# Factors split ahead, loads ordered behind the first gathers, row sums by halves: one change to a fused two-layer kernel

## The reference

```
s = L0_attn(xn)                      # spectral attention: normalise, cumsum, product
g = silu(L0_ffn(xn))                 # 64 experts, top 8, capacity 64, F = 96
x = x + s * g
xn = layernorm(x)
s = xn + lora_attention(rms(xn))     # 16 heads of 128, window 64, rotary
g = silu(L1_ffn(xn))                 # 16 experts, top 4, and a shared expert
x = x + s * g
```

```
h @ W.T + h @ A.T @ B.T * (1 / 16)   # rank 16; q, k, v and o
```

## Time and profile before

| | us |
|---|---|
| median of 3 runs | 1467.7 |
| lowest, highest | 1464.87, 1475.33 |
| the profiled execution, its time | 1472.05 |
| its span in the trace | 1470.0 |
| TensorE busy (share of the span) | 1215.2 (83%) |
| VectorE busy | 922.5 (63%) |
| ScalarE busy | 661.2 (45%) |
| GpSimd busy | 600.1 (41%) |
| mean granted clock of TensorE | 0.888 |

### The profile page before, as it was taken

How to read it: one execution, slowest core, us unless ns; L and a number is a source line. 1 busy time by engine, 2 the same in 40 slices (tenths; PEclk the granted TensorE clock), 3 DMA queues, 4 the chain that set the end, 5 groups by cost and what they waited for, 6 DMA issues and landing times.

```text
span 1470.0 us, 23570 instructions
## 1 busy us (share of the span) xinstructions
PE 1215.2 (83%) x6602; PEld 773.0 (53%) x6603; DVE 922.5 (63%) x2072; ACT 661.2 (45%) x1699; POOL 600.1 (41%) x629
## 2 busy tenths in 40 slices
PE   4836355996078999999989999899987999999786
PEld 3424232332045667667667666666764666664343
DVE  3867705566648867887886678777555444443535
ACT  1412123343254676567667555665644444443101
POOL 0378932552033433333333334343431444442744
PEclk9958575565589999999999999999998999999988
DMA  7176046974702212121201000003008233332422
GB/s 233 39 279 242 14 106 157 330 235 165 252 19 100 74 37 80 58 87 44 73 33 55 29 30 30 6 25 117 1 17 255 94 102 101 106 100 70 126 70 83
DMA packets 90999, 149.71 MB, mean 102 GB/s; under 512 B 10880, under 2 KB 63424, under 8 KB 88048
## 3 DMA queue, kind: packets, MB, share of 16 engines
q1 hardware_dynamic: 80928, 120.30, 24.6%
q0 software_dynamic: 9984, 28.32, 6.5%
HBM read 104.03 MB, written 44.56 MB: 101 GB/s over the span
## 4 chain that ended last, share of the span: by engine, by line
PE 49%; DVE 13%; issue 10%; POOL 6%; ACT 5%; DMA 5%; POOLq 5%; DVEq 3%; ACTq 2%; SPq 2%
PE ps L953 7%; PE ps L1027 5%; PE ps L1139 5%; PE ps L984 4%; PE ps L1151 3%; POOLq L2137 3%; PE ps L968 3%; PE ps L1149 2%; POOL wvo L2219 2%; PE ps L860 2%; PE ps L1009 2%; PE ps L1094 2%; PE ps L995 2%; DMA arena<-in_long 2%; PE ps L876 2%
## 5 line engine op out<-in xcount | busy, mean ns | idle before, releaser
L2180 POOL TENSOR_TENSOR arena<-arena 128x512 f32<-128x512 f32 x128 | 161.4, 1273 | 360.7 <-ACT arena L1371 360.1
L953 PE MATMUL ps<-arena 128*128 128x512 f16 x768 | 181.1, 387 | 0.0
L2185 POOL TENSOR_TENSOR arena<-arena 128x768 f32<-128x768 f32 x64 | 100.4, 1569 | 106.1 <-DVE arena L1819 106.1
L1370 ACT ACTIVATE arena<-ps 64x512 f32<-64x512 f32 x128 | 76.0, 594 | 134.4 <-DVE arena L1791 131.1
L1394 ACT ACTIVATE arena<-arena 128x192 f32<-128x192 f32 x256 | 113.1, 444 | 13.4 <-DVEq L1814 11.8
L953 PEld LDWEIGHTS ps<-arena 128*128 128x128 f16 x768 | 77.0, 102 | 79.8 <-issue 6.0
L1009 PE MATMUL ps<-arena 128*128 128x128 f32 x512 | 99.1, 297 | 14.8 <-ACT arena L1376 14.7
L1797 DVE TENSOR_TENSOR arena<-arena 128x512 f32<-128x512 f32 x128 | 107.0, 875 | 6.4 <-POOL arena L2180 6.4
L1791 DVE TENSOR_TENSOR arena<-ps,arena 128x512 f32<-128x512 f32 x128 | 85.3, 685 | 35.7 <-PE ps L953 34.8
L2206 POOL DMA_INDIRECT wvo<-xn_d,ic x80 | 77.5, 969 | 63.0 <-POOL ic L2203 63.0
L1027 PE MATMUL ps<-wvo,arena 128*128 128x256 f16 x768 | 91.2, 276 | 12.0 <-DVE arena L1974 7.7
(11 more groups left out here) (281 smaller groups left out, 2563.8 us busy)
## 6 DMA issues: line engine op xcount, KB each, us to landing
z_d<-wvo SPq DMA_DIRECT2D x4, 4096.0 KB, 27.7
arena<-z_d SPq DMA_DIRECT2D x16, 1024.0 KB, 5.6
arena<-wqk_d SPq DMA_DIRECT2D x16, 1024.0 KB, 5.0
arena<-in_wgu SPq DMA_DIRECT2D x32, 384.0 KB, 3.7
y_d<-wvo SPq DMA_DIRECT2D x80, 128.0 KB, 1.9
arena<-in_wdn SPq DMA_DIRECT2D x32, 192.0 KB, 4.4
arena<-in_w13T SPq DMA_DIRECT2D x4, 1408.0 KB, 12.3
wqk_d<-arena SPq DMA_DIRECT2D x4, 1024.0 KB, 4.0
```

The lines of the kernel that those rows point to most:

```text
L953: last = pe.matmul(ps[s][:, :], wqk[gg][:, s * DC + c, w, hh * DH:(hh + 1) * DH], hx[bb][:, :, x, c * P:(c + 1) * P], start=(c == 0 and w ...
L2180: nc.gpsimd.tensor_tensor(qk_s[:, s], qk_s[:, s], sin, ALU.mult).then_inc(sin_done, 1)
L2185: nc.gpsimd.tensor_tensor(a, a, ri.unsqueeze(2).to_broadcast([P, TPB, KW]), ALU.mult).then_inc(pn_done, 1)
```

## The change

It has four parts.

- **Factors.** The low-rank factors are loaded once, in stage 0, as 128 partitions of 1152 elements, and VectorE splits them there with two instructions. In stage 1 SP stores both parts to DRAM (long_d, short_d; four transfers). In stage 3 SP loads them in the layout that the products need, in three groups of 16 partitions, by six transfers of float16. stack_high, stack_again and stack_low are gone, and low_rank waits once, for the six transfers.
- **Order of the loads in stage 3.** SP waits for the third gather, then loads pair 4, then the factors, then pairs 5 and on.
- **Products while waiting.** TensorE does 16 products of 128x512 in bfloat16 at the start of stage 3; their result is not used.
- **Row sums.** Batch 0 has four buffers, so its four loads are issued at once; two of the buffers lie in space that stage 4 uses later (hx_f[1], wqk_f[1]). For that, the second group of weights is loaded after the fourth sum. A sum, for all 16 tiles, is three additions of 1024, 512 and 256 elements in place.

```diff
+            sp.dma_start(factors[:, 0:HALF], io["long"].rearrange("r (b n) -> (r b) n", b=2)).then_inc(lora_in, 16)
+            sp.dma_start(factors[:, HALF:NF], io["short"].rearrange("r (b n) -> (r b) n", b=2)).then_inc(lora_in, 16)
             sp.dma_start(wv_raw, io["wvT"].rearrange("(c p) n -> p c n", p=P)).then_inc(wvo_in, 16)
...
             stage_end(sp, 0)
+            for w in range(2):
+                sp.dma_start(long_d[w].rearrange("r (b n) -> (r b) n", b=2), factors16[:, w, 0:HALF]).then_inc(factors_kept, 16)
+                sp.dma_start(short_d[w].rearrange("r (b n) -> (r b) n", b=2), factors16[:, w, HALF:NF]).then_inc(factors_kept, 16)
...
             stage_end(sp, 2)
-            for j in range(WBUF // 2, WBUF):
-                load_experts(j)
-            sp.dma_start(short_raw, io["short"]).then_inc(lora_in, 16)
-            sp.dma_start(long_raw, io["long"]).then_inc(lora_in, 16)
-            for j in range(WBUF, PAIRS):
+            sp.wait_ge(gathered[2], 16)
+            load_experts(WBUF // 2)
+            for k, (long_part, short_part) in enumerate(((0, 0), (0, 1), (1, 0))):
+                rows = slice(k * RANK, (k + 1) * RANK)
+                sp.dma_start(long16[rows], long_d[long_part].rearrange("(q r) n -> r q n", q=4)).then_inc(factors_in, 16)
+                sp.dma_start(short16[rows], short_d[short_part].rearrange("(q r) n -> r q n", q=4)).then_inc(factors_in, 16)
+            for j in range(WBUF // 2 + 1, PAIRS):
                 load_experts(j)
...
             def load_rows(t):
-                seen(sp, mix_done, t - 2)
-                sp.dma_start(yg[:, t % 2], ...).then_inc(yg_in[t % 2], 16)
+                if t >= TPB:
+                    seen(sp, mix_done, t - 2)
+                landed = yg_first if 2 <= t < TPB else yg_in
+                sp.dma_start(rows_of(t), ...).then_inc(landed[t % 2], 16)
...
-            for t in range(2):
+            for t in range(TPB):
                 load_rows(t)
+            sp.wait_ge(wqk_out, 16 * NG)
+            load_group(0)
             for dst, name in ((cos, "cos"), (sin, "sin"), (mask0, "mask_first"), (mask1, "mask")):
                 sp.dma_start(dst, io[name]).then_inc(tabs_in, 16)
-            sp.wait_ge(wqk_out, 16 * NG)
-            for n in range(2):
-                load_group(n)
-            for t in range(2, TPB + 2):
+            seen(sp, mix_done, TPB - 1)
+            load_group(1)
+            for t in range(TPB, TPB + 2):
                 load_rows(t)
...
+            for _ in range(WARM):     # WARM = 16
+                pe.matmul(ps[7][:, :], ones_bf[:, :], ones_bf[:, :].unsqueeze(1).to_broadcast([P, 4, P]), start=True, stop=True)
             for j in range(3):
                 expert_rows(j)
...
+            dve.wait_ge(lora_in, 32)
+            nc.vector.tensor_scalar(factors16[:, 0], factors, UP_W, None, ALU.mult)
+            dve.drain()
+            nc.vector.scalar_tensor_tensor(factors16[:, 1], factors, UP_W, factors16[:, 0], ALU.mult, ALU.subtract)
             dve.wait_ge(w0_mm, 1)
...
             def summed(t):
                 u = t % 2
-                dve.wait_ge(yg_in[u], 16 * (t // 2 + 1))
-                nc.vector.tensor_reduce(mix[:, u], yg[:, u].rearrange("p k d -> p d k"), AX.X, ALU.add).then_inc(mix_done, 1)
+                a = rows_of(t)
...
+                nc.vector.tensor_tensor(a[:, 0:4], a[:, 0:4], a[:, 4:8], ALU.add)
+                dve.drain()
+                nc.vector.tensor_tensor(a[:, 0:2], a[:, 0:2], a[:, 2:4], ALU.add)
+                dve.drain()
+                nc.vector.tensor_tensor(mix[:, u], a[:, 0], a[:, 1], ALU.add).then_inc(mix_done, 1)
```

More of the change, by code:

```diff
@@ L28 @@
 WBUF = 8
+WARM = 16
 WGU, WDN = 2 * 2 * 2 * F0, 2 * 256
@@ L100, in build @@
         z_d = dram("z_d", (NT * K0 * P, D))
+        long_d = dram("long_d", (2, 4 * RANK, H1 * DH), F16)
+        short_d = dram("short_d", (2, 4 * RANK, D), F16)
         wqk_d = dram("wqk_d", (NG, P, 2 * DC * 512))
@@ L144, in build, with flat @@
         arena = sb("arena", [P, ARENA])
+        def flat(a):
+            return a.rearrange("p a b -> p (a b)")
         class Region:
@@ L268, in build @@
         yg_in = [sem(f"yg_in{u}") for u in range(2)]
+        yg_first = [sem(f"yg_first{u}") for u in range(2)]
         mix_done, g_ready, x1_done, xn2_ready = sem("mix_done"), sem("g_ready"), sem("x1_done"), sem("xn2_ready")
@@ L394, in build @@
         back = R1.take(P, DC, D)
+        R1.at = at_prod
+        NF = 4 * RANK * (H1 * DH + D) // P
+        factors = R1.take(P, NF)
+        factors16 = R1.take(P, 2, NF, dt=F16)
+        assert R1.at <= at_ohhi
         R1.at = 127 * 256
@@ L405, in build @@
         wqk_raw = R3.take(P, NG, 2, DC, 512)
-        R3.at = 512
-        long_raw = R3.take(3 * RANK, 4, H1 * DH)
         assert R3.at == 512 + 2 * UNITS * 512
@@ L416, in build @@
         y0 = R3.take(P, 4, D)
-        short_raw = R3.take(3 * RANK, 4, D)
         sums = R3.take(P, 4, 512)
@@ L492, in build @@
         hx = [R6.take(P, TPB, 2, 2 * D, dt=F16) for _ in range(2)]
+        yg_of = [yg[:, 0], yg[:, 1], flat(hx_f[1].rearrange("p a b c d -> p (a b c) d")).rearrange("p (k d) -> p k d", k=K0),
+                 wqk_f[1].rearrange("p (k d) -> p k d", k=K0)]
         R7 = Region()
@@ L558, in build, with rows_of @@
         CHUNK0 = T0 + 11
+        def rows_of(t):
+            return yg_of[t] if t < TPB else yg[:, t % 2]
         def tiles_at(table, h):
@@ L628, in _ @@
                 xn_stored.done(sp, NT - 2 + u, u)
+            sp.wait_ge(factors_kept, 16 * 4)
             stage_end(sp, 1)
@@ L666, in load_rows @@
             def load_rows(t):
-                seen(sp, mix_done, t - 2)
-                sp.dma_start(yg[:, t % 2], z_d[t * K0 * P:(t + 1) * K0 * P, :].rearrange("(k p) d -> p k d", p=P)).then_inc(yg_in[t % 2], 16)
+                if t >= TPB:
+                    seen(sp, mix_done, t - 2)
+                landed = yg_first if 2 <= t < TPB else yg_in
+                sp.dma_start(rows_of(t), z_d[t * K0 * P:(t + 1) * K0 * P, :].rearrange("(k p) d -> p k d", p=P)).then_inc(landed[t % 2], 16)
             def store_tile(t):
@@ L880, in low_rank @@
             def low_rank(n):
-                if n % UNITS == 0:
-                    pe.wait_ge(stack_ready, (1, 2, 4, 4)[n // UNITS])
+                if n == 0:
+                    pe.wait_ge(factors_in, 16 * 6)
                 seen(pe, lora_add, n - 1)
@@ L1290, in turned_out @@
                 nc.scalar.activation(hmT[:, j % 4], ps[6][0:F0, 0:P], ACT.Copy).then_inc(hmT_rd, 1)
-            def stack_high(q):
-                act.wait_ge(lora_in, 16 * 2)
-                nc.scalar.activation(short16[:, q], short_raw[:, q], ACT.Copy, scale=UP_W)
-                nc.scalar.activation(long16[:, q], long_raw[:, q], ACT.Copy, scale=UP_W).then_inc(stack_hi, 1)
-            def stack_again(q):
-                seen(act, stack_lo, q)
-                nc.scalar.activation(short16[0:RANK, q], short_raw[0:RANK, q], ACT.Copy, scale=UP_W).then_inc(stack_ready, 1)
             for j in range(3):
@@ L2238 @@
         "wqT": a["L1_attn_wq"].T, "wkT": a["L1_attn_wk"].T, "wvT": a["L1_attn_wv"].T, "woT": a["L1_attn_wo"].T,
-        "long": np.tile(np.stack([a["L1_attn_oA"], a["L1_attn_vB"].T, a["L1_attn_qB"].T, a["L1_attn_kB"].T], 1), (3, 1, 1)),
-        "short": np.tile(np.stack([a["L1_attn_oB"].T, a["L1_attn_vA"], a["L1_attn_qA"], a["L1_attn_kA"]], 1), (3, 1, 1)),
+        "long": np.concatenate([a["L1_attn_oA"], a["L1_attn_vB"].T, a["L1_attn_qB"].T, a["L1_attn_kB"].T], 0),
+        "short": np.concatenate([a["L1_attn_oB"].T, a["L1_attn_vA"], a["L1_attn_qA"], a["L1_attn_kA"]], 0),
         "gtT": np.concatenate([a["L1_ffn_gate_w"], a["L1_ffn_sgate_w"]], 0).T,
```

24 lines of the change are left out of this document (6 added, 18 removed).

## The result

The changed kernel takes 1452.49 us at the median of four runs (1448.42 to 1456.9), the kernel before 1471.51 beside it; the ratio is 0.9898, 95% interval 0.9852 to 0.9944. The forecast of 1444 us was a ratio of 0.9836 (1447.9 to 1472.05): the direction and the range held, and of the gain that was forecast (1.64%) the two sets show 62% and 88%. Two runs of the kernel before, in later sets, were slow ones and are left out throughout. The profiled run took 1454.3 us, its span is 1452.2, 17.8 less than the 1470.0 of before.

The account below looks back on a forecast made before the run. It took the late fifth gather, then TensorE at half clock, to bound stage 3. Terms 1 - 12.2 - 5.2 - 7.7 = -24.1 us gave 1447.9 in a run like the profiled one, 1444 at the median, range 1422 to 1460.

Parts of the forecast that it names:

- The bound and its place: Stage 3: TensorE stands 11.80 us for the late fifth gather, then bounds the pairs at half clock, 4.07 us each.
- the sign: Whole kernel: faster, -24.1 us in all; chance 0.77 of a gain over one per cent.
- the six pairs without the factors' copies: Stage 3, after the fifth gather's turn: 22.8 us instead of 27.96, -5.2.
- batch 0: Start of stage 4: four loads at once and shorter sums let normalising start near 389.8 instead of 397.52, -7.7 us.
- the warm products: Start of stage 3: sixteen products while TensorE waits cost 0, at most 1 us.
- the later sums: Stage 4, twelve row sums after the first batch: 0 us, -3 without contention, +8 with two or three on the path.
- Stages 0 and 1: Loading, splitting and storing the factors there costs +1 us (0 to +3).
- gather 4's: Stage 3, the fifth gather: rows turned at 221.0 instead of 233.16, -12.2 us (bounds -15 and -8).
- the lower bound of -8: Stage 3: if factors move as slowly per KB as before, 12.5 us from 212.4, the fifth gather lands near 225.
- The second rival: Stage 3: factor transfers, paced by partitions written, hold the queues from 212.4 to 250; slower, 1473 us; chance 0.06.
- The first rival: Stage 3: the clock comes up and stays, 22 pairs each 0.97 us faster, 21 us more gain, 1423; chance 0.17.
- The third: Stage 4: later additions and GpSimd block each other on the path, 25 us back, 1469, no change; chance 0.12.

Follow-up runs that it names:

- the two sets: The unedited changed kernel measured twice against the kernel before: ratio 0.9898 at first, 0.9855 when repeated in six runs.
- the repeated run: The changed kernel once more, unedited, in a later set of six runs beside the kernel before: 1449.13 us, ratio 0.9855.
- the first set: The changed kernel's first four runs, unedited, beside the kernel before: 1452.49 us, ratio 0.9898.
- the kernel with stacks of 48 rows: Changed kernel with factors kept in DRAM as a stack of three (six stores), read back in eight transfers to 48 partitions each: 1454.49 us, ratio 0.9888.

## Why the prediction was right, and where its size was off

*What was right.* The bound and its place (gather 4, then pairs on TensorE at half clock), the sign, and four terms to within a microsecond: the six pairs without the factors' copies took 22.80 us in the repeated run (forecast 22.8; 19.70 in the first trace, three of them at full clock by luck); batch 0 gave 7.9 (7.7), its additions took 1.23, 0.69 and 0.42 us (1.2, 0.7, 0.4); the warm products cost nothing; the later sums were worth nothing. On a gain of over one per cent, to which the prediction gave 0.77, the first set (1.02%, interval 0.56 to 1.48) does not decide; the repeated one (1.45%) reaches down to 0.90.

*Stages 0 and 1* cost nothing instead of 1 us: the loads landed in time, the four stores delayed the first row store by less than 1 us, and VectorE's first work of stage 1 starts at 31.37, before at 31.90.

*The term that was mis-sized is gather 4's*: -12.2 forecast, -8.7 and -7.8 measured, at the lower bound of -8. The step that fell short is "For gather 4 I take the 5.8 us median". That median holds for gathers among loads of one pair at a time. Its issue was forecast well (215.2, measured 215.89), but six factor transfers lay ahead of it, and it took 9.7 us. The bound by speed per KB, worked out beside it (12.5 us from 212.4, landing near 225), came within 1 us, in part by luck: the factors themselves took 10.5 us, from 213.36 to 223.87, and the gather landed 1.8 us behind them. Four kernels show what holds it: with pair 4 and the factors ahead TensorE waits 7.84 us, with four pairs ahead 6.24 us, with two pairs ahead 2.05 us, with the load of pair 4 alone not at all (2.9 us from issue to landing). What was issued before the gather sets its time, not the stage's median.

*The second rival* (transfers go by partitions written) was right that the shape matters and wrong in the size: 16 rows at a time do take 0.5 us a packet instead of 0.17, though whether the number of partitions does it is not shown; and the three pairs of them took 10.5 us, not 37.5, at a DMA share of 1.03 (219 to 224), that is with all engines at work.

*The first rival* (the clock comes up and stays) did not come true: stretches of 0 to 37 us at full clock between gather 4 and the last scatter, none that stayed. They blur the total by up to 8 us (123.0 us from gather 4's turn to the last scatter without any, 115.4 with 37). *The third* did not either, by the 167.3 and 167.5 us: additions and GpSimd do block each other, but not on the path there.

*The sum.* Against 24.1 us the profiled pair shows 17.8. Gather 4 is 3.5 of the 6.3 missing; the other 2.8 are the granted clock (+1.2 in stage 2, -3.1 and +4.3 in stage 3, +1.6 behind), less the 1 us that stages 0 and 1 did not cost and 0.2 that batch 0 gave more. The repeated run, luckier behind stage 3, shows 21.1.

## What to carry to other kernels

An early gather lands when what was issued before it has landed: in the six traces of these kernels that record both landings while transfers were under way, it landed 0.3 to 2.0 us after the last transfer issued ahead of it. So list the transfers between it and the event that releases it, add their own times, and move all but the ones that are due first behind it. Here that showed in the traces; its share of the whole kernel's time, 2 to 4 us, is hardly above the error. Do not price such a gather by the stage's median. Where runs of one kernel differ by 20 us with the granted clock, set each run's time beside its clock before reading a difference of 5 us, and take terms from stretches of the trace whose clock is the same in both.

## What the runs showed of the hardware

- Three transfers of 64 packets of 4096 bytes, each to 16 partitions, took 0.51 us a packet at the median in the changed kernel and 0.55 alone in the queues (138 GB/s in 177 to 182). As four transfers of 48 packets, each to 48 partitions, the same bytes took 0.17 us a packet, yet 17.5 us from the first packet to the last (212.8 to 230.3) instead of 6.7 (215.2 to 222.0).
- The first packet of gather 4 was served 7.1 us after its issue with one pair and six factor transfers ahead of it (changed kernel), 5.2 us with four pairs, 1.6 us with two pairs or one. In the kernel with stacks of 48 rows it was 1.6 us too, with packets of the factors served before and after it; why it was let in there and not in the changed kernel stays open.
- TensorE busy 5.00 of 5.00 us at clock 0.50, and 3.10 to 4.66 of 5.00 at 1.00, occur in one stage of one kernel; whether the clock came up there differed between two profiled runs of the same code.
- Within one kernel, the mean granted clock of a run tells its time to 2.5 us of scatter: 7.6 us for each 0.01 (129 runs).
